# One decoder on one core: two heads per search bank, one bank pool for mixed attention, causal masks after the exponential, and one DMA queue in the planner

## The chip, the cores and the metric

The kernel runs on one core of one Trainium2 chip, as one launch. The metric is the device time of that launch in microseconds. The engines are TensorE (PE; its weight loads are listed as PEld), VectorE (DVE), ScalarE (ACT), GpSimd (POOL) and SyncE (SP, which only issues transfers). Each engine runs its own instructions in the order in which the program emits them.

## The reference

A post-norm decoder of two layers over `x` of shape (4, 512, 256) with a context of (4, 1601, 128). Each line is `x = layernorm(x + f(x))` for one `f`: linear attention, mixed attention, grouped experts, a state-space block, a block `L1_xattn` with self and cross attention and their MLPs, and a scaled feed-forward. The change touches the attention softmax code, used by the second and fifth of these:

```python
# mixed attention, 16 heads of 16 channels, T = 512
att = where(tril(ones(T, T)), q @ k.T * scale, -inf)        # causal self attention
y = softmax(att) @ v
y = y + softmax(qc @ kc.T * scale) @ vc                      # cross attention over 1601 keys
out = y @ Wp + bp
# L1_xattn: 16 heads of 32 channels
a = softmax(q @ k.T * D ** -0.5)                             # self attention: a is masked AFTER softmax,
o = (a * (t > s)) @ v                                        # cross attention: not masked
```

## The kernel before

The program is written stage after stage: linear attention, mixed attention (tag `mx`), experts, state space, block attention `a1` (self), its MLP, block attention `a2` (cross), its MLP, scaled feed-forward. All products are fp32 or fp32r.

**Jobs.** An attention stage is a row of jobs, each for one batch element and four heads (`HG = 4`). The mixed stage has per batch element four self jobs (512 keys, causal) and four cross jobs (1601 keys), 32 in all. `a1` and `a2` have 16 jobs each. Keys come in cuts: one of 512 for self jobs, `KEY_CUTS` (384, 384, 384, 450) for cross jobs.

**Steps of a job.** `stack`: PE projects queries or keys, ACT writes the rounded part, DVE the rest, and (`split`) SP copies both parts to stacked tiles `qs` and `ks`. `peak` (the search, PE line 954): for 128 queries at a time PE makes the scores of a cut and DVE takes the row maximum (line 1104). `tops` and `turn_tops` (line 965) turn the maxima into two rows of the query stack, and `tops_turned` copies them there with a transfer. `weigh` (line 979): for 128 keys at a time PE makes scores less maximum, and ACT the exponential (line 1062) into a ring of tiles `p`. `values` (line 1012): PE multiplies `p` by the values into the bank `num`. In `a1` and `a2`, `weights` (line 1028) sums `p` by PE. Then `result`, `gather` (transfer into `thin`), `inverse` (DVE reciprocal, line 1127), `flat` and `spread` (transfers) and `quotient` (POOL, lines 1147 to 1152). The small transfers are issued by SP in `mx` and by ACT in `a1` and `a2`.

**Row tiles.** In `mx` a head needs 62 or 64 rows of PE's array, so `tiled = 2`: two matmuls run side by side, each on 64 rows, each into its own PSUM bank. In `a1` and `a2` `tiled = 1`.

**Banks.** Of the eight PSUM banks, `mx` gives four to the search as two twins (`self.twins`, a ring), three (4, 5, 7) to a pool `side` for `weigh`, `stack`, `turn_tops` and all the work beside attention, and one to `num`. In `a1` and `a2` search and `weigh` share one pool of six.

**Causal masks in `mx`.** After a search matmul of a self job, PE adds a bf16 tile `neg_a` of -1e30 to the diagonal block (line 958), and after a `weigh` matmul `neg_b` (line 985), both as full-array matmuls with an identity. In `a1` the exponential is multiplied instead by a 0/1 tile on POOL into `cut` (line 1161).

**The order.** `attention_steps` writes the order of all steps while the program is built. It keeps a clock for each engine (`Pace`), gives every possible next PE step a start time plus a penalty from `Policy`, and takes the lowest. Steps of other engines are put off until their inputs should be there. A transfer is reckoned as issue + size x `SENT` behind the queue's earlier transfers + `LANDING`, with a queue for each issuing engine. The real waits are semaphores; the estimates only set the order.

Of the kernel before, what the change touches and what calls it, by code (L numbers as in the profile page):

```python
# [11 lines left out]
ALU = mybir.AluOpType  # L12
# [13 lines left out]
KEY_CUTS = [(0, 384), (384, 384), (768, 384), (1152, 450)]  # L26
E = 8
# [39 lines left out]
Job = namedtuple("Job", "b g cuts first sub mask pairs summed nk add y vw q qb k kb q_after k_after values values_after shown y_after needs")  # L67
# [57 lines left out]
class Pace:  # L125
# [34 lines left out]
class Decoder:  # L160
    def __init__(self, nc, ctx, a, out):
# [5 lines left out]
        self.twins = [Bank(nc, ctx, psum[:, i:i + 2, :], f"{i}{i + 1}") for i in (0, 2)]  # L167
# [57 lines left out]
    def fence(self, *kept, running=()):  # L225
# [3 lines left out]
        flags = [*(f for name, f in self.flags.items() if name not in running), *(b.freed for b in self.banks + self.twins)]  # L229
# [340 lines left out]
    def attention_steps(self, jobs, q_slots, k_slots, tiled, before, during, beside, at_once, after, until, load, policy, rooms):  # L570

        side, search, places, raws, recs = rooms
        pace, ready, done, later = Pace(), defaultdict(float), set(), []
        for bank in self.banks + self.twins:
            bank.back_at = 0.0
# [10 lines left out]
        flow = [("peak", n, ci, j, i) for n, job in enumerate(jobs) for ci in range(len(job.cuts)) for j in range(parts) for i in range(TB)]  # L586
        after_job = [len(flow) - total for total in accumulate(parts * TB * len(job.cuts) for job in jobs)]
# [4 lines left out]
        queries = lambda n, kb: T - P * kb if jobs[n].mask == "causal" else T  # L592
        source = lambda n, ci: "q" if ci is None else ("k", ci)
# [50 lines left out]
        def candidates():  # L644
# [8 lines left out]
            if flow and ("split", *flow[0][1:3]) in done and (search is not side or len(side.idle) > 1):  # L653
                n, ci, *_ = flow[0][1:]
                yield start(narrow, max(ready["stack", n, None], ready["stack", n, ci], search.next().back_at, pace.free["dve"] - policy.dve_ahead)), policy.search if len(flow) > left() else policy.early_search, flow
# [28 lines left out]
        def account(due, kind, n, *at):  # L684
# [31 lines left out]
            elif kind == "peak":  # L716
                ci, j, i = at
                w = P * (i + 1) if job.mask == "causal" else job.cuts[ci][1]
                bank = self.took["peak", n, ci, j, i][0]
                end = pace.matmul(narrow, w * COLUMN + 14, max(ready["stack", n, None], ready["stack", n, ci], bank.back_at))  # L720
                if job.mask == "causal":
                    end = pace.matmul("full", tiled * 67, 0)
                bank.back_at = pace.run("dve", 75 + tiled * w / 0.96, end)
# [12 lines left out]
            elif kind == "weigh":  # L736
                kb, part = at
                w = queries(n, kb)
                for h in range(tiled * part, tiled * part + tiled):
                    bank = self.took["weigh", n, kb, h][0]  # L740
                    end = pace.matmul(narrow, w * COLUMN / tiled + 14, max(ready["tops", n], ready["stack", n, cut_of(n, kb)], bank.back_at))
                    if job.mask == "causal":
                        end = pace.matmul("full", 67, 0)
                    ready["weigh", n, kb, h] = bank.back_at = pace.run("act", 65 + w / 1.2, max(end, place_ready(n, kb, h)))
                    if job.mask == "upper":
                        ready["cut", n, kb, h] = pace.run("pool", 400, ready["weigh", n, kb, h])
# [87 lines left out]
    def softmax_attention(self, scope, tag, D, scale, jobs, cut_room, q_slots, k_slots, tiled, order, beside):  # L834
# [37 lines left out]
        tops = [(sb(f"mp{i}", [P, HG, TB, 4]), sb(f"top{i}", [P, HG, TB]), sb(f"mm{i}", [P, TB, tiled, 2, HT], F32R))  # L872
# [7 lines left out]
        if causal:  # L880
            neg_a, neg_b = sb("neg_a", [P, P], BF16), sb("neg_b", [P, P], BF16)
# [1788 lines left out]
```

## Time and profile before

| | |
|---|---|
| median of 3 runs | 3887.3 us (3878.41 to 3892.47) |
| the profiled execution | 3892.38 us, its span 3891.1 us |
| mixed attention, about | 190 to 1213 us |
| block attention a1, about | 1485 to 2000 us |
| block attention a2, about | 2142 to 3190 us |
| mean granted TensorE clock | 0.929 of 2.4 GHz |

The profile is one execution. Busy time counts datapath work; the ends of matmuls are modelled, so PE's busy time includes pipeline latency and short waits. An idle time in brackets stands before the instruction, with what ended it.

### The profile page before, as it was taken

Reading aid. Unit: us, or ns where it says so; the run is one execution under the profiler, and the core shown is the slowest. Engines: PE = TensorE matmul, PEld = TensorE weight load, DVE = VectorE, ACT = ScalarE, POOL = GpSimd, SP = SyncE. Lnnn points to the kernel's source line nnn. Section 1 sums busy time; section 2 is a strip of 40 time slices with the busy share of each in tenths; the row PEclk is TensorE's granted clock in tenths of the full one; section 3 lists DMA queues with packets and bytes.
Section 4 is the critical chain, followed back from the end, with each engine's and each line's share of the span. In section 5 each row is a group of like instructions: output and inputs, shape, how many; then the busy total and the mean of one; then the engine's idle time right before and its main releaser. Section 6 shows DMA issues by size and latency. Waiting matters only on the chain. (4 is left out here: it accounts for less than half of the span.)

```text
span 3891.1 us, 59054 instructions
## 1 busy us (share of the span) xinstructions
PE 3393.8 (87%) x22156; PEld 2132.0 (55%) x22156; DVE 2249.4 (58%) x4065; ACT 1675.6 (43%) x3067; POOL 981.0 (25%) x1030
## 2 busy tenths in 40 slices
PE   6789999999997957788867799999999987899998
PEld 3444444444435834455446555555555536787787
DVE  5768677686771366545445776676766615433432
ACT  1116657566573222334432255555455644222222
POOL 1110000000001023333334255555555553100000
PEclk9979999999998977899888799999999998999999
DMA  2022212212212215444420634343434302122211
GB/s 70 6 51 54 64 48 51 58 47 65 50 37 107 76 43 86 67 65 62 58 71 31 79 57 66 58 62 54 66 53 65 54 18 77 51 82 71 66 55 59
DMA packets 144627, 229.42 MB, mean 59 GB/s; under 512 B 40916, under 2 KB 90840, under 8 KB 141400
## 3 DMA queue, kind: packets, MB, share of 16 engines
q1 hardware_dynamic: 129048, 216.21, 26.9%
q10 hardware_dynamic: 15296, 9.45, 1.0%
q8 instruction: 177, 2.90, 0.3%
q14 instruction: 106, 0.87, 0.1%
HBM read 99.39 MB, written 8.91 MB: 28 GB/s over the span
## 5 line engine op out<-in xcount | busy, mean ns | idle before, releaser
L1104 DVE TENSOR_REDUCE a_mp<-bank 128x1 f32<-128x384 f32 (+2 forms) x1280 | 685.3, 590 | 400.0 <-PE bank L954 399.5
L1062 ACT ACTIVATE a_p<-bank 128x512 f32<-128x512 f32 (+1 forms) x1088 | 584.4, 600 | 514.7 <-PE bank L979 346.4
L1104 DVE TENSOR_REDUCE mx_mp<-bank 128x2 f32<-128x768 f32 (+4 forms) x640 | 588.7, 953 | 181.0 <-PE bank L954 105.0
L1062 ACT ACTIVATE mx_p<-bank 128x512 f32<-128x512 f32 (+3 forms) x1088 | 541.8, 558 | 318.0 <-PE bank L979 176.2
L1140 POOL TENSOR_TENSOR a_pair<-a_p 128x512 f32<-128x512 f32 x384 | 489.9, 1311 | 460.0 <-ACT a_p L1062 370.5
L954 PE MATMUL bank<-a_ks,a_qs 126*128 126x384 f32 (+2 forms) x1280 | 455.2, 397 | 52.6 <-ACT a_v L1985 22.3
L979 PE MATMUL bank<-a_qs,a_ks 128*128 128x512 f32 (+1 forms) x1088 | 468.0, 446 | 22.5 <-DVE a_yn L1860 5.3
L260 POOL TENSOR_TENSOR rs<-ve,neghalf 128x4 f32<-128x4 f32 (+2 forms) x80 | 78.3, 979 | 1098.8 <-DVE ve L255 1055.2
L979 PEld LDWEIGHTS bank<-a_qs,a_ks 128*128 128x128 f32 (+1 forms) x1088 | 206.6, 193 | 255.9 <-issue 169.2
L979 PE MATMUL bank<-mx_qs,mx_ks 64*128 64x512 f32 (+3 forms) x1088 | 304.1, 466 | 36.4 <-DVE mx_vc L1377 15.4
L954 PEld LDWEIGHTS bank<-a_ks,a_qs 126*128 126x128 f32 x1280 | 250.8, 197 | 132.7 <-DVE a_mp L1104 30.0
L1012 PE MATMUL bank<-a_p,a_v 128*32 128x256 f32 (+2 forms) x3840 | 271.0, 381 | 0.3
L954 PE MATMUL bank<-mx_ks,mx_qs 62*128 62x384 f32 (+4 forms) x1280 | 257.6, 397 | 12.1 <-DVE mx_mp L1104 9.4
L979 PEld LDWEIGHTS bank<-mx_qs,mx_ks 64*128 64x128 f32 (+1 forms) x1088 | 133.2, 184 | 239.6 <-issue 134.5
L1012 PE MATMUL bank<-mx_p,mx_vc 128*17 128x256 f32 (+1 forms) x3328 | 238.5, 386 | 2.1 <-ACT mx_raw L1068 2.1
L1161 POOL TENSOR_TENSOR a_cut<-a_p,a_upper 128x128 f32<-128x128 f32 x256 | 114.2, 461 | 292.0 <-ACT a_p L1062 289.7
L1147 POOL TENSOR_TENSOR mx_rec<-mx_raw,mx_rec 128x512 f32<-128x512 f32 x16 | 20.4, 1274 | 644.8 <-DMA mx_rec<-mx_flat 644.8
L1012 PEld LDWEIGHTS bank<-a_p,a_v 128*32 128x32 f32 (+1 forms) x3840 | 101.9, 109 | 137.0 <-issue 91.7
L954 PEld LDWEIGHTS bank<-mx_ks,mx_qs 62*128 62x128 f32 x1280 | 129.7, 189 | 83.5 <-DVE mx_mp L1104 44.0
L2404 DVE TENSOR_TENSOR sf_wl<-sf_raw,sf_wh 128x1024 fp32r<-128x1024 f32 x64 | 78.2, 1222 | 141.4 <-ACT sf_wh L2396 141.3
L1012 PEld LDWEIGHTS bank<-mx_p,mx_vc 128*17 128x17 f32 (+1 forms) x3328 | 68.1, 96 | 101.2 <-issue 63.9
L1028 PE MATMUL bank<-a_pair,ones 128*32 128x512 f32 x768 | 113.0, 633 | 0.0
(311 smaller groups left out, 5580.0 us busy)
## 6 DMA issues: line engine op xcount, KB each, us to landing
sf_raw<-in_h_w SPq DMA_DIRECT2D x64, 512.0 KB, 3.5
a_ks<-a_kh SPq DMA_DIRECT2D x96, 192.0 KB, 4.5
ex_w<-in_L_ffn_w SPq DMA_DIRECT2D x16, 1024.0 KB, 5.1
a_qs<-a_qh SPq DMA_DIRECT2D x64, 256.0 KB, 6.9
mx_ks<-mx_kh SPq DMA_DIRECT2D x192, 48.0 KB, 2.1
a_ks<-a_kl SPq DMA_DIRECT2D x48, 192.0 KB, 5.2
mx_qs<-mx_qh SPq DMA_DIRECT2D x128, 64.0 KB, 2.2
mx_rec<-mx_flat SPq DMA_DIRECT2D x128, 64.0 KB, 2.0
```

The source lines that it names most:

```text
L260: g.tensor_tensor(rs[0:np_, 0:n], ve[0:np_, 0:n], self.neghalf[0:np_, 0:n], ALU.pow).then_inc(*self.up("root", *key))
L954: m = pe.matmul(banks[r][:, 0:w], qs[r0:r0 + full - 2, j, P * i:P * i + P], ks[r0:r0 + full - 2, j, 0:w], start=True, stop=job.mask != "ca ...
L979: m = pe.matmul(bank[0:kp, q0:T], ks[r0:r0 + full, h // tiled, k0:k0 + kp], qs[r0:r0 + full, h // tiled, q0:T], start=True, stop=job.mask ...
L1012: m = pe.matmul(num[32 * h:32 * h + job.vw, q0:q1], val, src, start=kb == half == i == 0, stop=last, skip_group_check=True)
L1028: m = pe.matmul(self.bank("den", n)[32 * h:32 * h + 32, :], self.ones[0:src.shape[0], 0:32], src, start=first, stop=kb == nkb - 1, skip_gr ...
L1062: act.activation(probs[place % len(probs)][0:kp, q0:T], self.bank(part, n, kb, h)[0:kp, q0:T], ACT.Exp, scale=scale).then_inc(*self.frees( ...
L1104: v.tensor_reduce(best[:, tiled * j:tiled * j + tiled, i, ci], bank[:, 0:w] if tiled == 1 else bank[:, :, 0:w], AX.X, ALU.max).then_inc(*s ...
L1140: g.tensor_tensor(sums[h][:, :], even[:, :], odd[:, :], ALU.add).then_inc(*up("pair_made", n, kb, h))
L1147: g.tensor_tensor(rec[:, :], raw[:, :], rec[:, :], ALU.mult).then_inc(*up("quotient_made", n))
L1161: g.tensor_tensor(cut[place % len(probs)][:, :], probs[place % len(probs)][:, P * kb:P * kb + P], kept[:, :], ALU.mult).then_inc(*up("cut_ ...
L2404: v.tensor_tensor(lo[:, :, :], raws[t % 3][:, :, :], hi[:, :, :].bitcast(F32), ALU.subtract).then_inc(*up("weight_low", t))
```

## The change

- `MIXED_CUTS` (512, 512, 256, 322) replaces `KEY_CUTS` in `mx`. `pieces` divides each cut into pieces of at most 256 keys there (512 in `a1` and `a2`, where a piece is a cut as before).
- A search step of `mx` makes one piece of 128 queries for all four heads: two matmuls on each row tile, side by side in the halves of one bank. DVE reduces each of the two banks by itself over two heads. For a self job, pieces that lie wholly behind the diagonal are left out (6 steps, not 8).
- `self.twins` is gone; in `mx` all banks but the `num` bank form one pool of seven, from which a search step takes two.
- `neg_b` and the matmuls of line 985 are gone. POOL sets the part of `p` on the wrong side of the diagonal to zero, in place (`affine_select`), and `values` waits for that.
- The planner reckons all transfers in one queue, with `SENT` 0.0078 and `LANDING` 1100, and the policies have other numbers. `a1` and `a2` are touched by this alone.

```diff
-ISSUE, SENT, LANDING = {"sp": 610, "act": 500}, 0.0098, 900
+ISSUE, SENT, LANDING = {"sp": 610, "act": 500}, 0.0078, 1100
 Policy = namedtuple("Policy", "act_ahead dve_ahead values more_values totals more_totals search early_search turn stack beside aging rate lead")
-MIXED = Policy(700, 1100, 350, 200, -160, 140, -50, 600, 50, 60, 200, 100, 2.6, 4)
-OWN = Policy(700, 1100, 300, 200, -210, 90, 100, 600, -250, 60, 200, 100, 4.2, 2)
-CROSS = Policy(700, 1600, 300, 200, 90, 40, 100, 600, 50, 110, 200, 50, 5.2, 2.5)
+MIXED = Policy(900, 900, 350, 400, -160, 140, -50, 350, 50, -40, 200, 200, 2.6, 4.5)
+OWN = Policy(700, 1100, 300, 200, -160, 190, 150, 600, 200, -90, 200, 30, 4.2, 2.5)
+CROSS = Policy(700, 1600, 300, 200, 90, 40, 100, 600, 50, 110, 200, 30, 5.2, 2.5)
...
     def transfer(self, engine, size, ready):
         issued = self.run(engine, ISSUE[engine], ready)
-        self.free["queue", engine] = max(self.free["queue", engine], issued) + size * SENT
-        return self.free["queue", engine] + LANDING
+        self.free["queue"] = max(self.free["queue"], issued) + size * SENT
+        return self.free["queue"] + LANDING
+
+def pieces(cuts, wide):
+    return [(ci, c0, min(wide, w - c0)) for ci, (_, w) in enumerate(cuts) for c0 in range(0, w, wide)]
+
+def searched(job, s, i):
+    _, c0, w = job.pieces[s]
+    return max(0, min(w, P * (i + 1) - c0)) if job.mask == "causal" else w
...
-        side = Pool([*self.banks[0 if tiled == 1 else 4:5 if tiled == 1 else 6], self.banks[7]])
-        a_banks = side if tiled == 1 else Ring(self.twins)
+        side = Pool([*self.banks[0:5 if summed else 6], self.banks[7]])
...
-                bank = self.take(a_banks, part, n, *at)
-                banks = [bank] if tiled == 1 else [bank[:, r, :] for r in range(tiled)]
...
+                banks = [self.take(side, part, n, *at, r) for r in range(tiled)]
...
+                for k, head in enumerate(heads):
+                    for r, r0 in enumerate(base):
+                        m = pe.matmul(banks[r][:, T // 2 * k:T // 2 * k + w], qs[r0:r0 + full - 2, head, P * i:P * i + P],
+                                      ks[r0:r0 + full - 2, head, c0:c0 + w], start=k == 0, stop=not masked, skip_group_check=tiled > 1)
...
-                if job.mask == "causal":
-                    for h in heads:
-                        pe.matmul(self.bank(part, n, kb, h)[:, q0:q0 + P], self.identb[:, :], neg_b[:, :], start=False,
-                                  stop=True).then_inc(*self.fills(part, n, kb, h))
...
-                        pe.wait_ge(*self.freed("weigh", n, kb, h))
+                        pe.wait_ge(*(has("cut_made", n, kb, h) if job.mask == "causal" else self.freed("weigh", n, kb, h)))
...
+                        v.tensor_reduce(best[:, r:HG:tiled, i, s], bank.rearrange("p (k c) -> p k c", k=HT)[:, :, 0:w], AX.X, ALU.max
+                                        ).then_inc(*self.frees(part, n, *at, r))
...
+            elif part == "weigh" and job.mask == "causal":
+                kb, part_of = at
+                for h in range(tiled * part_of, tiled * part_of + tiled):
+                    corner = probs[weighed[n, kb, h] % len(probs)][:, P * kb:P * kb + P]
+                    g.wait_ge(*self.freed(part, n, kb, h))
+                    g.affine_select(out=corner, in_=corner, compare_op=ALU.is_ge, fill=0.0, base=0, pattern=[[1, P]],
+                                    channel_multiplier=-1).then_inc(*up("cut_made", n, kb, h))
```

## Rows read from the trace of the kernel before

**Rows 1.** Busy time by stage: us, then busy us (instructions) of each engine

```profile
core 0: us, PE busy (x) PEld busy (x) DVE busy (x) ACT busy (x) POOL busy (x), PEclk, DMA share, GB/s
190.00:1213.00 1023.00, 940.86 (x7664) 452.48 (x7664) 709.80 (x955) 587.59 (x1174) 91.00 (x85) 0.95 0.21 51
1485.00:2000.00 515.00, 411.33 (x2782) 263.22 (x2782) 239.93 (x462) 197.21 (x358) 176.15 (x325) 0.88 0.45 69
2142.00:3190.00 1048.00, 971.01 (x6956) 558.78 (x6955) 668.47 (x1373) 543.59 (x1021) 539.28 (x433) 0.96 0.39 57
```

**Rows 2.** Timeline of PE, 538 us: `weigh` and mask. Start us, us

```profile
538.12 0.39 PE L979 MATMUL bank<-mx_qs,mx_ks 64*128 64x256 f32 x2
538.45 0.28 PE L985 MATMUL bank<-mx_neg_b,identb 128*128 128x128 bf16 x2
538.66 0.47 PE L954 MATMUL bank<-mx_ks,mx_qs 62*128 62x450 f32 x2
```

**Rows 3.** Timeline of PE, 620 us: `weigh` without a mask

```profile
620.42 0.50 PE L979 MATMUL bank<-mx_qs,mx_ks 64*128 64x512 f32 x2
620.75 0.37 PE L954 MATMUL bank<-mx_ks,mx_qs 62*128 62x450 f32 x2
```

**Rows 4.** Timeline of PE, 232 us: search and mask

```profile
232.00 0.38 PE L954 MATMUL bank<-mx_ks,mx_qs 62*128 62x256 f32 x2
232.31 0.28 PE L958 MATMUL bank<-mx_neg_a,identb 128*128 128x128 bf16 x2
232.59 0.44 PE L954 MATMUL bank<-mx_ks,mx_qs 62*128 62x384 f32 x2
```

**Rows 5.** Timeline of PE, 604 and 1052 us: two search pairs, one pair

```profile
604.02 0.50 PE L979 MATMUL bank<-mx_qs,mx_ks 64*128 64x512 f32 x2 [1.07 <-DVE mx_xt L1362]
604.36 0.52 PE L954 MATMUL bank<-mx_ks,mx_qs 62*128 62x384 f32 x4
604.81 1.06 PE L1012 MATMUL bank<-mx_p,mx_vc 128*17 128x256 f32 x16
...
1052.08 0.34 PE L954 MATMUL bank<-mx_ks,mx_qs 62*128 62x384 f32 x2
1052.35 0.48 PE L281 MATMUL bank<-mx_xt,mx_Wcq 128*128 128x256 f32 x1
```

**Rows 6.** Waits of PE, 190 to 1213 us: total us, times, longest

```profile
PE bank L979 <- DVE mx_vc L1377: 15.4, 18, 1.0
...
PE bank L979 <- DVE mx_xt L1362: 6.4, 6, 1.1
PE bank L979 <- DVE mx_vs L1368: 5.5, 9, 0.8
...
PE bank L979 <- DVE mx_xb L1383: 1.6, 3, 0.9
```

**Rows 7.** Groups of DVE's reductions, 190 to 1213 us: busy us, mean ns

```profile
L1104 DVE TENSOR_REDUCE mx_mp<-bank 128x2 f32<-128x768 f32 x416 | 381.9, 951 | 106.7 <-PE bank L954 87.8 <-PE bank L958 17.6
L1104 DVE TENSOR_REDUCE mx_mp<-bank 128x2 f32<-128x900 f32 x128 | 135.3, 1090 | 19.0 <-PE bank L954 17.2
...
L1104 DVE TENSOR_REDUCE mx_mp<-bank 128x2 f32<-128x512 f32 x32 | 22.1, 690 | 15.5 <-PE bank L958 14.8
...
L1104 DVE TENSOR_REDUCE mx_mp<-bank 128x2 f32<-128x256 f32 x32 | 13.5, 421 | 21.0 <-PE bank L958 21.0
```

**Rows 8.** POOL: the affine selects, and who waited for a1's cuts

```profile
L895 POOL TENSOR_SCALAR_AFFINE_SELECT mx_neg_b<-mx_neg_b 128x128 bf16<-128x128 bf16 x1 | 0.3, 295 | 0.0
...
L902 POOL TENSOR_SCALAR_AFFINE_SELECT a_upper<-a_upper 128x128 f32<-128x128 f32 x1 | 0.3, 295 | 0.1
...
PE bank L1012 <- POOL a_cut L1161: 1.9, 2, 1.3
```

**Rows 9.** Timeline, 1667 to 1680 us in a1: a gather behind SP's transfers

```profile
1667.75 0.61 ACTq L1214 DMA_DIRECT2D a_thin<-a_rec  x1
1675.75 0.25 DVE L1127 RECIPROCAL a_thin<-a_thin 128x16 f32<-128x16 f32 x1 [5.42 <-DMA a_thin<-a_rec]
1676.47 1.08 ACT L1062 ACTIVATE a_p<-bank 128x512 f32<-128x512 f32 x2 [6.49 <-DVE a_thin L1127]
1679.95 1.22 PE L954 MATMUL bank<-a_ks,a_qs 126*128 126x512 f32 x2 [6.36 <-ACT a_v L1985]
```

**Rows 10.** Timeline, 1949 us in a1: a gather with SP's queue empty

```profile
1949.08 0.61 ACTq L1214 DMA_DIRECT2D a_thin<-a_rec  x1
...
1951.06 0.25 DVE L1127 RECIPROCAL a_thin<-a_thin 128x16 f32<-128x16 f32 x1 [10.16 <-DMA a_thin<-a_rec]
```

**Rows 11.** Waits in a1, 1485 to 2000 us: total us, times, longest

```profile
PE bank L965 <- DVE a_mm L1116: 35.6, 11, 5.4
PE bank L954 <- ACT a_v L1985: 17.5, 5, 9.0
...
DVE a_thin L1127 <- DMA a_thin<-a_rec: 70.0, 12, 12.0
```

**Rows 12.** The same wait in a2, 2142 to 3190 us

```profile
DVE a_thin L1127 <- DMA a_thin<-a_rec: 58.0, 5, 42.5
```

**Rows 13.** Timeline, 502 to 512 us in mx: a gather and its quotient

```profile
502.75 0.60 SPq L1214 DMA_DIRECT2D mx_thin<-mx_raw  x1
511.61 1.28 POOL L1147 TENSOR_TENSOR mx_rec<-mx_raw,mx_rec 128x512 f32<-128x512 f32 x1 [44.38 <-DMA mx_rec<-mx_flat]
```

More of the change, by code:

```diff
@@ L228, in fence @@
         nc = self.nc
[L229 removed]
+        flags = [*(f for name, f in self.flags.items() if name not in running), *(b.freed for b in self.banks)]
         for eng in (nc.tensor, nc.scalar, nc.vector, nc.gpsimd, nc.sync):
@@ L570, in attention_steps @@
     def attention_steps(self, jobs, q_slots, k_slots, tiled, before, during, beside, at_once, after, until, load, policy, rooms):
-        side, search, places, raws, recs = rooms
+        side, places, raws, recs = rooms
         pace, ready, done, later = Pace(), defaultdict(float), set(), []
-        for bank in self.banks + self.twins:
+        for bank in self.banks:
             bank.back_at = 0.0
@@ L585, in attention_steps @@
         stacks = [(n, ci) for n, job in enumerate(jobs) for ci in (None, *range(len(job.cuts)))]
-        flow = [("peak", n, ci, j, i) for n, job in enumerate(jobs) for ci in range(len(job.cuts)) for j in range(parts) for i in range(TB)]
-        after_job = [len(flow) - total for total in accumulate(parts * TB * len(job.cuts) for job in jobs)]
+        flow = [("peak", n, s, j, i) for n, job in enumerate(jobs) for s in range(len(job.pieces)) for j in range(HG if tiled == 1 else 1)
+                for i in range(TB) if searched(job, s, i)]
+        after_job = [max(at for at, step in enumerate(flow) if step[1] == n) + 1 for n in range(len(jobs))]
+        after_job = [len(flow) - end for end in after_job]
         last_of = {step[1]: step for step in flow}
@@ L716, in account @@
             elif kind == "peak":
[L717 to L720, printed above, removed]
-                if job.mask == "causal":
-                    end = pace.matmul("full", tiled * 67, 0)
-                bank.back_at = pace.run("dve", 75 + tiled * w / 0.96, end)
+                s, j, i = at
+                w, ci, heads = searched(job, s, i), cut_at(n, s), HG // tiled if tiled > 1 else 1
+                banks = [self.took["peak", n, *at, r][0] for r in range(tiled)]
+                end = pace.matmul(narrow, heads * (w * COLUMN + 14), max(ready["stack", n, None], ready["stack", n, ci], *(bank.back_at for bank in banks)))
+                if on_diagonal(job, s, i):
+                    end = pace.matmul("full", tiled * heads * 67, 0)
+                for bank in banks:
+                    bank.back_at = pace.run("dve", 75 + heads * w / 0.96, end)
             elif kind == "tops":
@@ L942, in pe_part @@
             elif part == "peak":
-                ci, j, i = at
-                w, ks = P * (i + 1) if job.mask == "causal" else job.cuts[ci][1], kst[k_slot[n, ci]]
-                if j == i == 0:
+                s, j, i = at
+                ci, c0, _ = job.pieces[s]
+                w, ks, heads = searched(job, s, i), kst[k_slot[n, ci]], [j] if tiled == 1 else range(HT)
+                if c0 == j == i == 0:
                     if n < q_slots:
@@ L1085, in dve_part @@
             best, top, both = tops[n % 2]
-            cuts = len(job.cuts)
+            cuts = len(job.pieces)
             if part == "split" and job.first:
@@ L1891, in job @@
             return Job(
-                b=b, g=h, cuts=KEY_CUTS if cross else [(0, T)], first=True, sub=0, mask=None if cross else "upper",
+                b=b, g=h, cuts=KEY_CUTS if cross else [(0, T)], pieces=pieces(KEY_CUTS if cross else [(0, T)], T), first=True, sub=0, mask=None if cross else "upper",
                 pairs=cross, summed=True, nk=nk, add=False, y=ys[b % len(ys)][:, h, :], vw=D,
```

84 lines of the change are left out of this document (45 added, 39 removed).

## The prediction

> **What bounds the kernel now.** I read the busy times by stage first, for the three stages that the change can touch [rows 1]. The reader is to see that in mixed attention (1023 us) no engine but PE is near full: PE is busy 92%, DVE 69%, ACT 57%, POOL 9%. PE works in order, so what it spends there, streaming, draining or waiting, is the stage's time. Then I read PE's timeline there, start to start, since busy times of matmuls overlap. Last come the waits by stage. In a1 PE is busy only 80% of 515 us and gets 0.88 of the 2.4 GHz clock; in a2 it is busy 93% [rows 1].
>
> **The masks of `weigh` (gain).** A `weigh` pair of 256 columns, its two mask matmuls and the next pair start at 538.12, 538.45 and 538.66 us: 0.54 us from pair to pair [rows 2]. Without a mask a pair of 512 columns takes 0.33 us to the next [rows 3]. Half the columns stream 256/2.4 = 0.107 us less, so 0.22 us. The mask costs PE 0.54 - 0.22 = 0.32 us. There are 16 self jobs x 4 key blocks x 2 head pairs = 128 groups: **-41 us**. Its bounds: only the mask's own 0.21 us (-27), and 0.4, the dearer mask of the next term (-51).
>
> **The masks of the search (gain).** A search pair with its mask takes 0.59 us for 256 columns [rows 4]. A pair in a run of pairs takes 0.45 - 0.27 = 0.18 us for 384 [rows 5], so some 0.13 for 256. A mask group costs about 0.45. The matmuls stay 256, but in 64 groups of four, not 128 of two: 64 x (0.45 - 0.13 for two more mask matmuls) = -20 us. That row is from the stage's start, where little else can run, so I take less: **-12 us**, bounds 0 and -20.
>
> **More, shorter search pairs (loss).** A cross job had 4 cuts x 4 query blocks x 2 = 32 pairs; it gets 7 pieces x 4 x 2 = 56. A self job goes from 8 to 12. That is 16 x 24 + 16 x 4 = 448 pairs more for the same columns. Each adds what a pair costs beside its stream: 0.18 - 0.16 = 0.02 us [rows 5], or, if the pair can't get shorter than 0.18 us because its weights load no faster, 0.18 - 0.107 = 0.07. So 9 to 33 us; the second pair of a step goes to the same banks and waits for no one, hence near the low end: **+13 us**.
>
> The Trainium skill (TensorE: Matmul & The Clock Gate, LDWEIGHTS, and Part 3, The mechanism) has a weight load take its columns over 1.2 GHz, 107 ns here, and overlap running matmuls only in another row group. That speaks against the change: with every load exposed the 448 pairs would cost 48 us in place of 13. The trace does not bear out the whole of it, since 0.18 us is less than 0.16 + 0.107.
>
> **Banks (gain).** A `weigh` pair needs two of three side banks. When a projection, transpose or value product holds one, PE waits for DVE to empty it, as at 604.02 us [rows 5]. Such waits of line 979 sum to 15.4 + 6.4 + 5.5 + 1.6 = 28.9 us [rows 6]. With seven banks most should go: **-25 us**. Bounds: 0, if searches take up the new banks, and -29.
>
> **DVE (hidden).** Reductions of the 512 form take 0.69 us, of 768 0.951, of 900 1.09 [rows 7]. A cross job goes from 24 x 0.951 + 8 x 1.09 = 31.5 to 48 x 0.69 + 8 x some 0.3 = 35.5 us, +64 us over 16 jobs. A self job has now two of each form (256, 512, 768, 1024 elements), 6.5 us, and gets 4 x 0.421 + 8 x 0.69 = 7.2: +11. The maximum over pieces, now in self jobs too, adds some 8. DVE goes from 710 to about 790 us of a stage that shrinks to 960: 82%. I put it at nothing, hidden by its 313 idle us; without that cover it costs up to 80.
>
> **The cut on POOL (loss).** 256 affine selects at 0.295 us [rows 8] are 76 us for a POOL that is 91% idle in this stage. PE's `values` now waits for them: if PE had nothing else, four in a row delay each of the 64 self blocks by at least the last one and its signal, some 0.4 us, 26 us in all. But a1 has the same arrangement with a slower cut, and PE waits for it 1.9 us [rows 8]. I take **+6**, bounds 0 and 26. Behind the waiting `values` on PE stand the next searches and `weigh` pairs, and behind those ACT and DVE.
>
> Cuts of other widths move the same bytes in as many transfers, so SP is at nothing. Mixed attention: -41 - 12 + 13 - 25 + 6 = **-59 us**.
>
> **One queue in the planner, a1 (gain).** ACT issues a gather at 1667.75 us while SP's transfers of queries and keys are under way. It lands for DVE at 1675.75, 8.0 us later; with SP's queue empty it is 2.0 us [rows 9, 10]. The planner reckoned about 1.5 us and put the reciprocal on DVE and the next issue on ACT that early. So DVE stands 5.4 us, ACT 6.5 and PE 6.4 [rows 9]. PE's waits for line 965 (35.6 us) and for ACT's value copies (17.5) are mostly this; so are 48 of DVE's 70 us, the last two waits (10.2 and 12.0) being the tail [rows 10, 11]. Six split transfers of 262144 bytes at 0.0078 ns are 12.3 us in the new queue, so a gather behind them is now expected late and its users are put behind other work. Of the 53 us some 4 belong to the first job. I take 60% of the other 49, since the other policy numbers shift too: **-30 us**. Bounds: 0 and -60, the latter with some clock given back: a1 runs at 0.88 against 0.95 in mx [rows 1].
>
> The Trainium skill (DMA: Bandwidth & Descriptors, Queues, rings and completion order) says that an SDMA engine takes turns between queue rows packet by packet. By that a small transfer on ACT's row need not sit out SP's backlog, and one queue in the planner would be the worse picture and this term 0. The 8.0 against 2.0 us disagrees.
>
> **a2.** The gather wait is 58.0 us, but 42.5 is the last job's [rows 12]. There is no such stall to remove: **0**, bounds -10 and +10 for the new order.
>
> **Sum.** -59 - 30 + 0 = -89 us on the profiled 3892.4, so 3803. That run is 5 us over the median of the runs; against 3887.3 the same change gives 3798. I say 3800.
>
> **The rivals.**
>
> *One half pays.* (a) The shorter pairs can't beat 0.18 us (+33, not +13) and DVE or POOL shows through (+26, not +6): mixed -59 + 40 = -19, total -49, **3838**. For it: DVE at 82% with its waits for PE in between. Against: the second pair of a step needs no bank of its own. (b) The stalls of a1 stay, because the gather is planned before the splits are reckoned: total -59, **3828**. For it: the OWN policy changes in seven numbers, which may undo the order. Against: in rows 9 the gather comes after SP's splits.
>
> *Nothing comes out.* The new order loses in each stage what the parts gain: **3887**. For it: the planner's penalties are guesses for a machine that it doesn't model. Against: removed matmuls are gone in any order.
>
> *Slower: cuts behind a late quotient.* POOL's queue is in order. A self job's cuts stand behind the previous job's quotient, which waits for four transfers. If that is late, `values` on PE is late, and the whole stage with it. By the planner's numbers gather to quotient is 1.77 + 0.32 + 1.77 + 4.05 = 7.9 us; the trace shows 8.9 [rows 13]. A delay of 1 us is harmless; this decides only from (89 + 12)/16 = 6.3 us in each of 16 self jobs. At 7 us the time is 3892 - 89 + 112 = 3915, or **3910** by the median. For it: POOL was idle so far, so lateness was never priced. Against: a1 lives with the same order.
>
> **Chances and range.** Both halves (-50 to -142 us): 0.52, its own range 3745 to 3837. One half (-12 to -50): 0.30. More than -142: 0.03. Nothing: 0.06. Slower: 0.09. A measurement of this kernel tells about 0.3% (12 us) from nothing. Faster 0.85, same 0.06, slower 0.09. The range takes the first two and leaves out 0.18: 3745 to 3865. Its low end is the sum of the good bounds held to what ACT and DVE allow (mixed -90, a1 -50); its high end lets a1 give nothing and mixed a third.
>
> **What would show it.** Line 985 gone, and `weigh` of self blocks followed within 0.25 us by the next pair. Mixed attention near 965 us, a1 near 485, a2 unchanged within 10. Waits of line 979 for `mx_vc`, `mx_xt` and `mx_vs` near zero. DVE's wait for `a_thin` in a1 below 30 us, most of it in the last two jobs. PE's wait for POOL's cuts below 10 us. Long waits of PE or DVE inside mx, or pairs of 256 columns 0.18 us apart, would make it wrong.

## The result, and the profile after

The changed kernel takes 3748.7 us (median of 4 runs, 3746.7 to 3751.2), against 3888.4 us (4 runs, 3878.4 to 3892.5) before: a ratio of 0.9645, with a 95% interval of 0.9625 to 0.9664. The profiled execution has a span of 3749.9 us, 141 less than before. The forecast was 3800. One of the four executions of the fifth experiment below, the masks of `weigh` back on PE, took 14125 us and is left out of its time.

The first view is the busy time by stage, now cut exactly: a stage runs from its first projection on PE (`mx_xt,mx_Wq`, `a_xn,a_wq`) to that of the next stage (`ex_xa,ex_w`, or the transposes of `ma_xh`). In the kernel before, with the columns of [rows 1]:

```profile
182.70:1228.60 1045.90, 952.49 (x7697) 460.80 (x7697) 717.83 (x980) 591.87 (x1180) 93.33 (x89) 0.94 0.21 52
1481.20:1989.50 508.30, 410.89 (x2777) 262.91 (x2778) 236.44 (x459) 191.34 (x352) 176.15 (x325) 0.89 0.44 64
```

and in the changed kernel:

```profile
179.30:1147.50 968.20, 877.65 (x8337) 475.53 (x8337) 740.87 (x1460) 574.36 (x1180) 163.46 (x344) 0.94 0.23 57
1399.60:1843.40 443.80, 388.33 (x2776) 246.55 (x2776) 238.50 (x459) 191.34 (x352) 177.36 (x325) 0.96 0.50 73
...
1988.60:3065.00 1076.40, 986.28 (x7007) 570.70 (x7007) 675.92 (x1391) 545.38 (x1025) 544.15 (x437) 0.95 0.39 56
```

Mixed attention fell by 77.7 us (forecast 59) and a1 by 64.5 (forecast 30). a2, cut in the same way, was 1073.2 and is 1076.4: +3 (forecast 0). The two account for all of the gain. The 965 us that the prediction named for mixed attention was 1023 less 59, and 1023 was a rough window; from the exact 1045.9 the same forecast gives 987, so the 968.2 is not a hit. Read span less PE's busy time as PE standing. In mixed attention it hardly moved: 93.4 before, 90.6 after. What fell there is PE's busy time, by 74.8 us, although PE has 640 instructions more. In a1 standing fell from 97.4 to 55.5 us, and busy time by 22.6 with the same work, at a granted clock of 0.96 of 2.4 GHz in place of 0.89.

PE's timeline in the changed kernel, for [rows 2, 3, 5]:

```profile
262.69 0.28 PE L1002 MATMUL bank<-mx_qs,mx_ks 64*128 64x256 f32 x2
262.90 0.63 PE L1029 MATMUL bank<-mx_p,mx_vs 128*17 128x256 f32 x8
...
560.28 0.50 PE L1002 MATMUL bank<-mx_qs,mx_ks 64*128 64x512 f32 x2 [0.94 <-DVE mx_xt L1393]
560.62 0.40 PE L972 MATMUL bank<-mx_ks,mx_qs 62*128 62x256 f32 x4
560.86 0.39 PE L1002 MATMUL bank<-mx_qs,mx_ks 64*128 64x512 f32 x2
561.18 0.62 PE L1029 MATMUL bank<-mx_p,mx_vc 128*17 128x256 f32 x8
561.74 0.50 PE L972 MATMUL bank<-mx_ks,mx_qs 62*128 62x256 f32 x4
562.17 0.62 PE L1029 MATMUL bank<-mx_p,mx_vc 128*17 128x256 f32 x8
```

`weigh` is line 1002 now. A pair of 256 columns is followed after 0.21 us, where it took 0.54 with its mask. The search is line 972: two pairs of 256 columns take 560.86 - 560.62 = 0.24 us, so 0.12 us each against 0.107 of streaming. That is a step with row-tiled work on both sides, which 78 of the 448 steps of this shape are, without an idle time in them. Between full-array work, as from 561.74 us on, 168 of the 448 take a median of 0.43 us, and the mean of all 448 is 0.40 us. The 0.94 us wait at 560.28 is of the same kind as the 1.07 us of [rows 5].

### The profile page after: what moved, and what is told of

Its sections match the earlier page's. It is cut to its first block and busy times, and to the rows that moved or that the text cites. A ratio compares the mean times of both kernels' runs of the same rounds, so it can differ in the third digit from the quotient of the medians.

```text
span 3749.9 us, 61606 instructions
## 1 busy us (share of the span) xinstructions
PE 3292.2 (88%) x22796; PEld 2129.6 (57%) x22796; DVE 2274.6 (61%) x4545; ACT 1657.2 (44%) x3067; POOL 1052.8 (28%) x1284
## 5 line engine op out<-in xcount | busy, mean ns | idle before, releaser
L1125 DVE TENSOR_REDUCE mx_mp<-bank 128x2 f32<-128x512 f32 (+2 forms) x1088 | 611.6, 621 | 108.0 <-PE bank L972 67.4
L1079 ACT ACTIVATE mx_p<-bank 128x512 f32<-128x512 f32 (+3 forms) x1088 | 523.9, 572 | 273.2 <-PE bank L1002 272.1
L972 PE MATMUL bank<-a_ks,a_qs 126*128 126x384 f32 (+2 forms) x1280 | 452.0, 398 | 39.9 <-ACT a_v L2016 9.4
L972 PEld LDWEIGHTS bank<-a_ks,a_qs 126*128 126x128 f32 x1280 | 248.5, 196 | 122.6 <-DVE a_mp L1123 28.9
L972 PEld LDWEIGHTS bank<-mx_ks,mx_qs 62*128 62x128 f32 x2176 | 182.4, 194 | 186.8 <-issue 134.8
L972 PE MATMUL bank<-mx_ks,mx_qs 62*128 62x256 f32 (+2 forms) x2176 | 257.1, 318 | 33.5 <-ACT mx_p L1079 7.8
L1029 PE MATMUL bank<-mx_p,mx_vc 128*17 128x256 f32 (+1 forms) x3328 | 247.7, 390 | 1.0 <-ACT mx_raw L1085 1.0
L1002 PE MATMUL bank<-mx_qs,mx_ks 64*128 64x512 f32 (+3 forms) x1088 | 223.6, 429 | 13.6 <-DMA mx_qs<-mx_mt 7.1
L1002 PEld LDWEIGHTS bank<-mx_qs,mx_ks 64*128 64x128 f32 (+1 forms) x1088 | 103.0, 188 | 109.0 <-issue 71.2
L1182 POOL TENSOR_SCALAR_AFFINE_SELECT mx_p<-mx_p 128x128 f32<-128x128 f32 x256 | 71.0, 294 | 190.8 <-ACT mx_p L1079 185.9
```

The costliest lines, as they stand in the source:

```text
L972: m = pe.matmul(banks[r][:, T // 2 * k:T // 2 * k + w], qs[r0:r0 + full - 2, head, P * i:P * i + P], ks[r0:r0 + full - 2, head, c0:c0 + w] ...
L1002: pe.matmul(bank[0:kp, q0:T], ks[r0:r0 + full, h // tiled, k0:k0 + kp], qs[r0:r0 + full, h // tiled, q0:T], start=True, stop=True).then_in ...
L1029: m = pe.matmul(num[32 * h:32 * h + job.vw, q0:q1], val, src, start=kb == half == i == 0, stop=last, skip_group_check=True)
L1079: act.activation(probs[place % len(probs)][0:kp, q0:T], self.bank(part, n, kb, h)[0:kp, q0:T], ACT.Exp, scale=scale).then_inc(*self.frees( ...
L1125: v.tensor_reduce(best[:, r:HG:tiled, i, s], bank.rearrange("p (k c) -> p k c", k=HT)[:, :, 0:w], AX.X, ALU.max).then_inc(*self.frees(part ...
L1182: g.affine_select(out=corner, in_=corner, compare_op=ALU.is_ge, fill=0.0, base=0, pattern=[[1, P]], channel_multiplier=-1).then_inc(*up("c ...
```

## The experiments

All times below are medians; lengths of stages and waits are from the profiled execution of each. The kernel before had 3879.6 us beside the first four experiments, 3882.8 beside the next four and 3884.2 beside the last four. A stage's length is cut as above.

**One queue alone.** The kernel before with `SENT`, `LANDING` and `transfer` of the changed kernel, its policies kept.

```diff
-ISSUE, SENT, LANDING = {"sp": 610, "act": 500}, 0.0098, 900
+ISSUE, SENT, LANDING = {"sp": 610, "act": 500}, 0.0078, 1100
...
-        self.free["queue", engine] = max(self.free["queue", engine], issued) + size * SENT
-        return self.free["queue", engine] + LANDING
+        self.free["queue"] = max(self.free["queue"], issued) + size * SENT
+        return self.free["queue"] + LANDING
```

> The kernel before, with only the planner's transfer estimate of the changed kernel (one queue, 0.0078, 1100); all policies, banks and masks as before. Theory (the stalls of a1 come from gathers that the planner expects too early): a1 shortens by 40 to 64 us and mixed attention moves by less than 10, so 3825 to 3850. Rival (the new policy numbers did it): a1 stays within 10 us of 508, total within 12 us of 3888.

Measured: 3836.3 us, ratio 0.9878 (0.9856 to 0.99). In a1:

```profile
1478.00:1927.90 449.90, 392.06 (x2777) 246.43 (x2778) 237.84 (x459) 193.12 (x352) 177.50 (x325) 0.96 0.50 72
```

508.3 became 449.9 us, and mixed attention moved by 1 us. PE's wait for `a_mm` fell from 35.6 to 9.2 us. The queue estimate makes 58 of the 64.5 us of a1. The edit changes two constants with the queue. They move the landing that the planner reckons for a gather of 8 KB by 0.2 us only, but they were not run alone.

**Two queues in the changed kernel.** The reverse edit, with all else of the change.

```diff
-ISSUE, SENT, LANDING = {"sp": 610, "act": 500}, 0.0078, 1100
+ISSUE, SENT, LANDING = {"sp": 610, "act": 500}, 0.0098, 900
...
-        self.free["queue"] = max(self.free["queue"], issued) + size * SENT
-        return self.free["queue"] + LANDING
+        self.free["queue", engine] = max(self.free["queue", engine], issued) + size * SENT
+        return self.free["queue", engine] + LANDING
```

> The changed kernel with the old transfer estimate (a queue for each engine, 0.0098, 900). Theory: a1 loses most of its 64 us again, 3790 to 3815. Rival (policies did it): under 3765. A third possibility is that the estimate also carries part of the gain in mixed attention, where SP issues everything: then mixed is longer than 968 us by over 10.

Measured: 3806.6 us, ratio 0.981 (0.9795 to 0.9824). a1 went back to 507.4 us, with mixed attention at 970.8. So a1 and mixed attention are two separate gains, and the new OWN policy is worth nothing without the new estimate.

**Old policies.** The changed kernel with all three policies of before.

```diff
-MIXED = Policy(900, 900, 350, 400, -160, 140, -50, 350, 50, -40, 200, 200, 2.6, 4.5)
-OWN = Policy(700, 1100, 300, 200, -160, 190, 150, 600, 200, -90, 200, 30, 4.2, 2.5)
-CROSS = Policy(700, 1600, 300, 200, 90, 40, 100, 600, 50, 110, 200, 30, 5.2, 2.5)
+MIXED = Policy(700, 1100, 350, 200, -160, 140, -50, 600, 50, 60, 200, 100, 2.6, 4)
+OWN = Policy(700, 1100, 300, 200, -210, 90, 100, 600, -250, 60, 200, 100, 4.2, 2)
+CROSS = Policy(700, 1600, 300, 200, 90, 40, 100, 600, 50, 110, 200, 50, 5.2, 2.5)
```

> The changed kernel with the three old rows of policy numbers. Theory (structure and queue estimate carry the gain): 3750 to 3775. Rival (the numbers carry it): 3800 or more, most of it in a1 (OWN differs in seven numbers).

Measured: 3828.6 us, ratio 0.9865 (0.9848 to 0.9881). a1 took 451.2 us, so its policy is worth 7 us. Mixed attention took 1038.7, hardly less than before: here my theory fell. The windows of mixed attention and the waits of PE in it:

```profile
181.20:1220.00 1038.80, 909.25 (x8337) 485.75 (x8337) 737.56 (x1457) 580.19 (x1180) 163.83 (x343) 0.93 0.21 52
```

```profile
PE bank L972 <- ACT mx_p L1079: 24.2, 65, 1.0
```

PE stands 129.5 us against 90.6, and is busy 31.6 us longer. The search now waits for exponentials to empty its banks (24.2 us, 65 times; 7.8 us, 25 times with the new numbers). With one pool search and `weigh` compete for banks, and who is let ahead of whom decides. These waits are 16.4 us of the 70; the rest is spread over other waits and busy time.

**Two pools.** The changed kernel with its banks divided as before: four for the search, three for the rest.

```diff
-        side = Pool([*self.banks[0:5 if summed else 6], self.banks[7]])
+        side = Pool([*self.banks[0:5], self.banks[7]] if summed else [*self.banks[4:6], self.banks[7]])
+        search = side if summed else Pool(self.banks[0:4])
...
```

> The changed kernel with mixed attention's banks divided as before: three for weigh, projections and side work, four for searches (two to a step). All else as changed, the planner's rule for taking a search step adapted. Theory of the prediction (waits for side banks were worth 25 us): mixed attention longer by 15 to 30 us, 3765 to 3780. Rival, from the trace after, which still has PE waiting some 23 us for DVE to empty banks of side work: the number of banks was not what these waits came from, and the time stays within 8 us of 3749.

Measured: 3803.0 us, ratio 0.9792 (0.9766 to 0.9818). Mixed attention took 1017.8 us, 50 more than with one pool. That is more than my theory (15 to 30) and far from the rival (none). Some 18 us of it are at the stage's start. There, with three banks, the projections of values wait for DVE one after another. PE's timeline before:

```profile
198.77 2.08 PE L281 MATMUL bank<-mx_Wv,mx_xt 128*128 128x256 f32 x4 [7.30 <-DVE mx_vs L1368]
201.36 2.08 PE L281 MATMUL bank<-mx_Wv,mx_xt 128*128 128x256 f32 x4 [0.52 <-DVE mx_vs L1368]
...
223.69 1.12 PE L281 MATMUL bank<-mx_Wcv,mx_ctx 128*65 128x256 f32 x2 [0.78 <-DVE mx_vc L1377]
224.74 0.47 PE L954 MATMUL bank<-mx_ks,mx_qs 62*128 62x128 f32 x2
```

and in the changed kernel:

```profile
186.71 3.72 PE L297 MATMUL bank<-mx_Wv,mx_xt 128*128 128x256 f32 x16 [1.55 <-POOL mx_neg_a L910]
190.27 1.03 PE L297 MATMUL bank<-mx_Wcv,mx_ctx 128*128 128x256 f32 x4
195.36 7.69 PE L297 MATMUL bank<-mx_Wcv,mx_ctx 128*128 128x256 f32 x22 [4.06 <-DVE mx_vs L1399]
202.98 0.44 PE L972 MATMUL bank<-mx_ks,mx_qs 62*128 62x128 f32 x4
```

The first search starts 224.7 - 182.7 = 42.0 us into the stage before, 203.0 - 179.3 = 23.7 after, and 223.4 - 181.4 = 42.0 with two pools. The waits are only part of it. Before, groups of four of these matmuls take 2.08 us (0.52 each); sixteen take 3.72 us (0.23 each) after. The granted clock of the two stretches, before and after, has both levels:

```profile
198.00:224.70 26.70, 19.68 (x38) 10.87 (x38) 6.10 (x11) 0.00 (x0) 7.87 (x9) 0.50 0.11 26
```

```profile
186.70:203.00 16.30, 12.23 (x44) 9.66 (x44) 11.62 (x18) 0.00 (x0) 15.11 (x16) 0.79 0.39 94
```

0.50 is the lower level, 1.2 GHz: PE, stopped for DVE after each group, stayed there for the whole stretch. With two pools the stretch 197.4 to 223.4 us has 0.50 as well.

The other 32 us are not in waits. The 1088 matmuls of `weigh` take 228.3 us with two pools and 197.9 with one, each counted from its start to the start of PE's next matmul, and the idle time behind them is the same (12.6 and 13.2 us). With one pool 672 of them are followed by another `weigh` matmul, with two pools 541. A `weigh` matmul takes 0.06 us to the next `weigh` matmul and 0.33 to a value product, so each pair that is set behind another saves PE time.

**Masks of `weigh` back on PE.** The changed kernel with the `neg_b` matmuls of before; `values` waits for ACT alone.

```diff
-                    pe.matmul(..., start=True, stop=True).then_inc(*self.fills(part, n, kb, h))
+                    m = pe.matmul(..., start=True, stop=job.mask != "causal")
+                if job.mask == "causal":
+                    for h in heads:
+                        pe.matmul(self.bank(part, n, kb, h)[:, q0:q0 + P], self.identb[:, :], neg_b[:, :], start=False,
+                                  stop=True).then_inc(*self.fills(part, n, kb, h))
...
```

> The changed kernel with the weigh masks of self jobs back on PE (two bf16 matmuls behind each pair), none on POOL. Theory (a mask group costs PE 0.32 us, 128 groups): the self blocks of the mixed stage take 8 to 12 us more each, mixed attention 35 to 50 us more than 968, total 3782 to 3800. Rival (the self blocks got shorter by the shared banks and the order, PE has slack there): under 3765.

Measured: 3780.6 us, ratio 0.9752 (0.9732 to 0.9771): 32 us more than the changed kernel. Its three executions spread over 19 us, 3770.9 to 3789.6, so the 32 are uncertain by some 10. The profiled execution, the fastest, has mixed attention at 992.1, 24 us more, where I had expected 35 to 50. `weigh` and its masks alone, counted from start to next start, take 42.9 us more; 11.2 us came back in the search, whose waits got shorter, and the rest in small amounts elsewhere.

**Masks of `weigh` on POOL in the kernel before.** The same part alone, the other way; the mask matmuls are taken out and `values` waits for the cut.

```diff
...
+            elif part == "weigh" and job.mask == "causal":
...
+                    g.affine_select(out=corner, in_=corner, compare_op=ALU.is_ge, fill=0.0, base=0, pattern=[[1, P]],
+                                    channel_multiplier=-1).then_inc(*up("cut_made", n, kb, h))
```

> The kernel before with only the weigh masks moved to POOL; old banks, cuts, policies, queue estimate. Theory: the same 41 us come out here, 3830 to 3855 where the kernel before takes 3880. Rival (they come out only with the shared banks): within 12 us of the kernel before.

Measured: 3845.7 us, ratio 0.991 (0.9895 to 0.9925), so -37 us, and -39.9 in the profiled mixed attention. `weigh` with its masks takes 42.6 us less here, counted from start to next start. Both ways the masks are thus worth the 41 us of the term on PE; what the whole kernel keeps of it was 37 us here and 32 there.

**The planner told of side banks.** In the changed kernel's waits in mixed attention (below, in the part on banks) PE still stands for DVE's copies of side work, though seven banks are there. The planner notes when a bank comes free (`back_at`) for searches and `weigh`, but not for work beside attention. It takes such a bank for empty the moment it was taken. This edit tells it the end of that work.

```diff
...
+        self.fresh.append(bank)
...
                     due = pace.matmul("full", ns, due) if engine == "pe" else pace.run(engine, ns, due)
+                for bank in self.fresh:
+                    bank.back_at = due
+                self.fresh.clear()
```

> The changed kernel, and the planner also told when a bank taken by side work (projections, transposes, value products, output) comes free; before, it kept the old time of that bank and so gave it to the next pair at once. Theory (PE's remaining waits for DVE in front of pairs come from this, some 23 us in mixed attention, and some in a1 and a2): those waits nearly vanish, mixed attention 10 to 25 us shorter, total 3715 to 3740. Rival (the waits move elsewhere, the policies having been set with them): within 8 us of 3749.

Measured: 3685.2 us, ratio 0.9497 (0.9483 to 0.9511), 63.5 us under the changed kernel, more than I had expected. Mixed attention took 930.5 us, a1 422.5, a2 1070.7. This version is faster than both kernels. Its mixed attention, and PE's longest waits there for the query stack, for exponentials and for a side copy:

```profile
181.20:1111.70 930.50, 862.05 (x8337) 468.26 (x8337) 735.99 (x1456) 574.59 (x1180) 163.87 (x343) 0.96 0.24 59
```

```profile
PE bank L1007 <- DMA mx_qs<-mx_mt: 8.6, 9, 4.3
...
PE bank L977 <- ACT mx_p L1084: 6.9, 24, 0.5
...
PE bank L298 <- DVE mx_vs L1404: 2.5, 1, 2.5
```

No `weigh` (line 1007) or search (line 977) waits for a side copy any more; what is left of that kind is a projection's (line 298).

**The cut three times.** The changed kernel, each cut made three times over in sequence on POOL.

```diff
-                    g.affine_select(...).then_inc(*up("cut_made", n, kb, h))
+                    for _ in range(3):
+                        g.affine_select(...).then_inc(*up("cut_made", n, kb, h))
+                        g.wait_ge(*has("cut_made", n, kb, h))
```

> The changed kernel with each of the 256 cuts on POOL done three times in a row, each waiting for the one before, the planner not told: the cost of one goes from 0.29 to about 1.0 us. Theory (the cut is well covered): POOL gets 16 x 1.0 = 16 us of cuts in a self job of 12 us, so it becomes the bound there and shows how far the cover goes: 40 to 110 us slower, all of it in self blocks, with PE waiting on POOL. If the self blocks lengthen by less than 5 us each, POOL has much more room than I reckon. Rival (already one cut per head is on the path): the loss is above 2 x 0.3 x 256 = 150 us.

Measured: 3856.7 us, ratio 0.9934 (0.992 to 0.9949), 108 us over the changed kernel, and mixed attention (1078.6) is 110 longer. The cuts' line in the view by source line, and who waits, first here:

```profile
L1183 POOL TENSOR_SCALAR_AFFINE_SELECT mx_p<-mx_p x768: 284/295/1583, 235.6 to 1078.9; 128x128 f32<-128x128 f32 x192
...
  PEld bank L1029: 84.3, 111
  PE bank L1029: 37.5, 65
```

then in the changed kernel:

```profile
L1182 POOL TENSOR_SCALAR_AFFINE_SELECT mx_p<-mx_p x256: 282/292/514, 232.3 to 971.5; 128x128 f32<-128x128 f32 x128
...
  PEld bank L1029: 0.9, 4
```

Once, the cut is hidden. At three times its length PE's matmuls stand 37.5 us for it and its weight loads 84.3.

**New MIXED numbers in the kernel before.** Nothing else is changed.

```diff
-MIXED = Policy(700, 1100, 350, 200, -160, 140, -50, 600, 50, 60, 200, 100, 2.6, 4)
+MIXED = Policy(900, 900, 350, 400, -160, 140, -50, 350, 50, -40, 200, 200, 2.6, 4.5)
```

> The kernel before with nothing changed but the policy numbers of mixed attention, taken from the changed kernel. Theory: the numbers fit the seven-bank pool and the two-head search; with twins and three side banks they give little: within 15 us of before, all in mixed attention. Rival: the numbers are what was gained, and structure only came along; then mixed attention falls by 50 to 70 us, as it rose by 70 us when the changed kernel got the old numbers back.

Measured: 3907.3 us, ratio 1.0052 (1.0037 to 1.0068), slower by 20 us, 18 of them in mixed attention. The numbers are no gain of their own.

**Half of the old numbers, and the other half**, in the changed kernel:

```diff
-MIXED = Policy(900, 900, 350, 400, -160, 140, -50, 350, 50, -40, 200, 200, 2.6, 4.5)
+MIXED = Policy(700, 1100, 350, 200, -160, 140, -50, 350, 50, -40, 200, 200, 2.6, 4.5)
```

> The changed kernel with three of the new numbers of mixed attention set back: act_ahead 900 to 700, dve_ahead 900 to 1100, more_values 400 to 200. Theory: more_values is what kept PE from making value products in small bites and changing its tiling each time, so this half carries most of the 70 us: 3790 to 3815. Rival: it carries under 20 us, below 3770, and the other numbers carry the rest.

```diff
-MIXED = Policy(900, 900, 350, 400, -160, 140, -50, 350, 50, -40, 200, 200, 2.6, 4.5)
+MIXED = Policy(900, 900, 350, 400, -160, 140, -50, 600, 50, 60, 200, 100, 2.6, 4)
```

> The changed kernel with the other five new numbers of mixed attention set back: early_search 350 to 600, stack 60 for -40, aging 200 to 100, lead 4.5 to 4 (beside and the rest were the same). Theory: under 30 us, 3750 to 3780. Rival: an early search is what fills PE while the exponentials of a cross job are behind, so this half carries most of the 70 us: 3790 to 3820.

The second edit sets back four numbers, not five as its expectation says. Measured: 3761.0 us (ratio 0.9683, 0.9662 to 0.9704) and 3778.1 us (0.9726, 0.9703 to 0.9749), 12 and 29 us over the changed kernel. In mixed attention the halves cost 11.6 and 23.0 us, 35 together, and both at once 70.5. The first half does not carry the loss, as I had thought; each costs more when the other is set back too. Which single number matters most was not tried.

**The told planner in the kernel before.** The edit of the seventh experiment, with twins, three side banks and all else of before.

> The kernel before, with the planner told when work beside attention gives its bank back (it was never told; the same edit took 63 us from the changed kernel, 38 in mixed attention and 21 in a1). Theory: the 28.9 us of line 979's waits for mx_vc, mx_xt, mx_vs and mx_xb in mixed attention are this and not the number of banks: they go, mixed attention falls by 20 to 35 us and a1 by 10 to 25, in all 3825 to 3860. Rival: with three side banks the planner knows better and has no other bank to give: mixed attention falls by under 10 us.

Measured: 3809.3 us, ratio 0.981 (0.9788 to 0.9833), 75 us under before. Mixed attention:

```profile
177.90:1180.70 1002.80, 945.81 (x7697) 461.56 (x7697) 717.36 (x980) 591.33 (x1180) 93.66 (x89) 0.96 0.22 54
```

PE stands 57.0 us there, not 93.4, with the same three banks. a1 took 483.4 and a2 1063.1 us. The gain is more than my theory's: 75 us where it had 25 to 60, and 43 in mixed attention where it had 20 to 35. PE's timeline at the stage's start, with the last value projections and the first search:

```profile
195.87 7.57 PE L282 MATMUL bank<-mx_Wcv,mx_ctx 128*128 128x256 f32 x26
203.37 0.33 PE L959 MATMUL bank<-mx_ks,mx_qs 62*128 62x128 f32 x2
```

The first search starts 203.4 - 177.9 = 25.5 us into the stage, 42.0 before, with three side banks in both. So the late start was the planner's doing as well: 16.5 of the 43 us are there. These few lines, which leave the work of every engine as it was, give more than half of what the whole change gives.

## Why the prediction came out as it did

The direction, the mechanisms of the masks and of the queue, and the range held. The sum was 89 us where 140 were measured. The measured 3748.7 lies only 4 us inside the range, whose low end stood on at most -50 in a1, where 64.5 came; that it held is in part luck.

The table adds up, for mixed attention, the time from the start of each matmul of PE to the start of the next, by kind. A kind is thus charged with the wait and the change of tiling behind it, so the table says where the time is, and the experiments say why.

| us | before | changed | masks to POOL in before | masks back on PE | two pools | told planner in before |
|---|---|---|---|---|---|---|
| `weigh` and its masks | 269.3 | 197.9 | 226.7 | 240.8 | 228.3 | 270.3 |
| search | 215.1 | 215.7 | 213.9 | 204.5 | 219.1 | 219.5 |
| masks of the search | 30.8 | 24.4 | 30.9 | 23.7 | 25.3 | 32.0 |
| value projections | 89.6 | 60.5 | 89.7 | 61.0 | 82.7 | 50.4 |
| value products | 279.7 | 303.8 | 280.3 | 296.5 | 296.2 | 276.1 |
| the rest | 161.4 | 165.9 | 164.5 | 165.7 | 166.2 | 154.5 |

By the steps of the prediction:

**The masks of `weigh` (-41): right.** 0.54 us became 0.21 from pair to next on the path, 0.33 against the 0.32 taken. In the table the masks are 42.6 us one way and 42.9 the other. The part alone gave the kernel 37 us and cost 32 to undo, cut included.

**More, shorter pairs (+13): the size was too high, and the cost per pair the wrong unit.** 1280 search matmuls took 215.1 us before and 2176 take 215.7 now, so 448 more pairs cost about 1 us. A pair does not have one price: a step of two pairs takes 0.24 us amid row-tiled work and 0.43 between full-array work. The cost beside the stream was largely the change of tiling, and two pairs of a step now share one. The prediction's sign of being wrong, pairs of 256 columns 0.18 us apart, did come (the second pair starts a median of 0.22 us after the first), but it did not mean a loss. The rule of the Trainium skill (TensorE: Matmul & The Clock Gate, LDWEIGHTS and Part 3), by which a load of 107 ns is exposed or overlaps only in another row group, would have made 48 us with every load exposed. The trace sides with the overlap; the two matmuls of a pair are on different row tiles.

**The cut on POOL (+6): right.** PE's weight loads waited 0.9 us for it, and its matmuls have no wait for it. It would not have stayed free for long: three times the length brings 108 us. The slower rival, cuts behind a late quotient, has no such wait in the trace.

**DVE (0): right, though its busy time was reckoned too high.** The forecast had 790 us of DVE. There are 896 reductions of 512 elements, as counted, and DVE is busy 740.9 us of 968.2 (77%). The 896 at 0.683 us would be 612 us, but they overlap in the trace and together cover 559.1:

```profile
L1125 DVE TENSOR_REDUCE mx_mp<-bank 128x2 f32<-128x512 f32 x896 | 559.1, 683 | 86.7 <-PE bank L972 63.7 <-PE bank L980 19.9
...
L1125 DVE TENSOR_REDUCE mx_mp<-bank 128x2 f32<-128x132 f32 x128 | 29.5, 290 | 4.1 <-PE bank L972 3.8
```

**Banks (-25): the step that failed.** The prediction said that `weigh` waits for DVE's side copies because two of three banks are needed, and that with seven "most should go". PE's waits in mixed attention of the changed kernel:

```profile
PE bank L972 <- DVE mx_xb L1414: 7.6, 12, 0.8
...
PE bank L972 <- DVE mx_vs L1399: 5.4, 9, 0.7
PE bank L1002 <- DVE mx_xt L1393: 5.2, 6, 1.0
...
PE bank L972 <- DVE mx_vc L1408: 4.7, 3, 1.7
```

They sum to 22.9 us where 28.9 were [rows 6], and 17.7 of them now stand before the search. The cause was not the number of banks but that the planner handed out a bank that a side copy still held. The last experiment shows it: with three banks and a told planner, one entry of 1.3 us is left of PE's `weigh` waits for these tiles, and the stage is 43 us shorter:

```profile
PE bank L984 <- DVE mx_xb L1388: 1.3, 2, 0.7
```

The banks do gain 50 us under this planner, but elsewhere. 18 are at the start of the stage, where PE no longer stops after each group and the clock is granted earlier; a told planner gets 16.5 of these with three side banks too. The rest is in `weigh`, 30.4 us in the table, where pairs follow each other more often. The policy numbers were left as they are for one pool, and two pools with a told planner were not run, so how much of the 50 needs seven banks stays open.

**The policies: not costed at all.** The prediction put them at nothing, with a word on the planner's penalties in a rival. In mixed attention 70 us hang on them, in both directions: the new structure with the old numbers gives 7 us, the old structure with the new numbers loses 18. They belong to the structure and can't be priced apart from it. A reader of the diff would have had to count them into the range; the rival "nothing comes out" (3887) came closest to that picture, with the planner as its cause.

**The search masks (-12): half of it in the trace.** The same 256 mask matmuls take 24.4 us in the table, 30.8 before: 6 us. No experiment tests them by themselves.

**One queue, a1 (-30): right in kind, half in size.** The 64.5 us are more than the bound of 60. The step took 60% of 49 us of standing. PE's standing fell by 97.4 - 55.5 = 41.9 us. The other 22.6 us are busy time: the same 2777 matmuls at 0.96 in place of 0.89 of 2.4 GHz. The clock stood in the text as a bound, "with some clock given back", and should have been a term, since [rows 1] had the one stage with much standing at the lowest clock. The waits in a1, for [rows 11]:

```profile
DVE a_thin L1151 <- DMA a_thin<-a_rec: 45.5, 9, 12.3
...
PE bank L972 <- ACT a_v L2016: 4.5, 6, 0.8
...
PE bank L988 <- DVE a_mm L1140: 3.6, 2, 3.3
```

35.6 and 17.5 us of PE became 3.6 and 4.5. I had said that DVE's wait for `a_thin` would be below 30 us; it is 45.5. That was wrong: most of the gain came although DVE still waits, since PE no longer stands behind it. A gather with SP's transfers before it, as in [rows 9], now looks like this:

```profile
1558.04 0.61 SPq L1228 DMA_DIRECT2D a_ks<-a_kl  x1
...
1563.47 0.61 ACTq L1245 DMA_DIRECT2D a_thin<-a_rec  x1
1564.13 1.57 ACT L1079 ACTIVATE a_p<-bank 128x512 f32<-128x512 f32 x3 [0.26 <-PE bank L972]
1566.50 2.07 ACT L1079 ACTIVATE a_p<-bank 128x512 f32<-128x512 f32 x4 [0.79 <-PE bank L1002]
1569.05 0.24 DVE L1151 RECIPROCAL a_thin<-a_thin 128x16 f32<-128x16 f32 x1
```

The reciprocal comes 5.6 us after the gather, with no idle time before it, and ACT has made seven exponentials in between. The rule of the Trainium skill (DMA: Bandwidth & Descriptors, Queues, rings and completion order), by which queue rows take turns packet by packet, would have made this edit worth nothing. It made 58 us, so for this kernel one queue is the better picture; how the transfers share the engines, no run shows.

**Mixed attention in sum.** It came to -77.7 us where -59 were forecast. By the table `weigh` with its masks gives 71.4, of which the masks are some 43. The value projections give 29.1 and the masks of the search 6.4. The search costs 0.6, the value products cost 24.1, which the prediction had at nothing, and the rest costs 4.5. Of the 24.1, 8.5 are idle time behind the value products; the cause of the others stays open. The term for the banks had a size near to some of this, with a cause that is not the one the runs show; that is luck.

**a2 (0): right**, +3.

## What to carry to other kernels

When an order is planned ahead, look for what the planner is not told (a bank still held, a queue shared) before adding resources: its blind spot shows as many short waits on things that had a free alternative. A stall on PE can cost more than its length (here 42 us of standing went together with 23 us of busy time), so price the clock when a stall goes. Numbers that were fitted to a structure are part of it: test a change of structure with its own numbers, and don't read a failure with the old ones as the structure's.

## What the runs showed of the hardware

Two 256-column pairs on two row tiles, issued together, take 0.24 us with row-tiled work on both sides, weight loads included, and 0.43 us between full-array work. An `affine_select` of 128 x 128 fp32 on POOL takes 0.29 us, as the bf16 one did; one on each tile costs PE 0.9 us of waits in all, three in sequence cost the kernel 108 us. A small transfer on ACT's queue behind SP's large ones landed after 8.0 us, and after 2.0 with SP's queue empty [rows 9, 10], and a planner that reckons both in one queue orders a1 better by 58 us. And a granted clock of 0.50 held for the 26.7 us in which PE stopped for some 0.5 to 0.8 us after each group of four matmuls.
